# A fourth scan bank, a ring for the scan state, one block in place of two, weight turns moved, and new start and end orders

## The reference

```python
# image: patches of 16x16x3, layernorm, W, layernorm -> 196 tokens; txt gives 77 more
y = _layernorm(p, ln1_g, ln1_b)
y = jnp.einsum('bnf,fe->bne', y, W) + bias
h = jnp.concatenate([_layernorm(y, ln2_g, ln2_b), txt], axis=1)      # (32, 273, 256)
# recurrence over every second token (137 steps), state (B, 256, 64)
x_sub = x[:, ::2] * rsqrt(mean(x_sub ** 2) + 1e-6) * g_norm          # x = _layernorm(h)
x_proj, gate = jnp.split(jnp.einsum('bld,ed->ble', x_sub, w_in) + b_in, 2, axis=-1)
def step(h, xt):
    h = jnp.tanh(h * A + xt[:, :, None] * Bm)
    return (h, h @ c_sum + Dv * xt)                                    # c_sum = Cm.sum(axis=0)
out = einsum(ys * silu(gate), w_out) + b_out                           # then each row twice
h = h + out
# feed-forward on layernorm(h), int weights scaled by 1/127
return h + einsum(silu(einsum(x, wg)) * einsum(x, wu), wd)
```

## Time and profile before

| | us |
|---|---|
| median of 3 runs | 1422.66 (1420.58 to 1423.19) |
| the profiled execution | 1424.49 |
| its span, first to last instruction | 1422.6 |
| until the first `grow` | 77.2 |
| from there to the last `squash` | 1270.6 |
| from there to the end | 74.8 |

### The profile page before, as it was taken

The page is one execution under the profiler, slowest core; times in us unless marked ns, Lnnn a source line. Parts: engine busy times, 40 slices in busy tenths (PEclk is TensorE's granted clock), DMA queues, the critical chain, the costliest instruction groups (busy, mean ns, idle before and its releaser), DMA issues.

```text
span 1422.6 us, 25915 instructions
## 1 busy us (share of the span) xinstructions
PE 1248.4 (88%) x7199; PEld 642.3 (45%) x7199; DVE 1079.0 (76%) x2401; ACT 1010.4 (71%) x1955; POOL 439.5 (31%) x443
## 2 busy tenths in 40 slices
PE   3858899999999999999999999999889989988865
PEld 1623345454545454545444445454344444433333
DVE  4638788888878787878787878787888888878621
ACT  1446786868686868787878786877877778768612
POOL 5303152515161615242424343423212122121121
PEclk8769999999999999999999999999999999999987
DMA  7230414141414142332324141303232232231210
GB/s 184 65 66 19 112 29 115 32 112 33 109 33 109 45 97 62 80 78 64 88 54 104 38 111 31 98 7 108 56 89 72 55 105 56 65 81 53 53 52 7
DMA packets 154926, 100.52 MB, mean 71 GB/s; under 512 B 129088, under 2 KB 143296, under 8 KB 153536
## 3 DMA queue, kind: packets, MB, share of 16 engines
q1 hardware_dynamic: 154880, 99.95, 28.1%
HBM read 58.85 MB, written 41.06 MB: 70 GB/s over the span
## 4 chain that ended last, share of the span: by engine, by line
PE 36%; issue 22%; ACT 12%; DVE 9%; DMA 8%; POOL 6%; SPq 3%; ACTq 0%; DVEq 0%; POOLq 0%
PE U L1114 7%; PE Y L1124 7%; DVE U L693 5%; ACT h L881 4%; PE P L1259 4%; DMA y_scr<-y_fx 4%; PE P L1260 4%; PE P L1199 3%; PE P L1168 3%; PE P L1274 2%; PE P L1275 2%; DMA yT<-y_scr 2%; POOL raw_s L1006 2%; DVE act L810 2%; SPq L582 1%
## 5 line engine op out<-in xcount | busy, mean ns | idle before, releaser
L693 DVE TENSOR_TENSOR U<-h,a_col 128x512 f32<-128x512 f32 x1096 | 722.6, 690 | 182.4 <-ACT h L881 175.9
L881 ACT ACTIVATE h<-U 128x512 f32<-128x512 f32 x1096 | 626.9, 598 | 221.3 <-PE U L1114 216.8
L1114 PE MATMUL U<-x_diag,b_st 128*128 128x512 f16 x1096 | 389.8, 387 | 80.7 <-DVE U L693 68.3
L1124 PE MATMUL Y<-h,read_st 128*32 128x512 f32 x2192 | 296.5, 613 | 0.3 <-ACT h L881 0.3
L1114 PEld LDWEIGHTS U<-x_diag,b_st 128*128 128x128 f16 x1096 | 104.9, 99 | 336.3 <-DVE U L693 275.8
L1056 POOL TENSOR_TENSOR xT_act<-act,xT_act 128x448 f16<-128x448 f32 x120 | 127.7, 1071 | 196.8 <-ACT xT_act L965 196.7
L1168 PE MATMUL P<-tok_w,xT_act 128*112 128x256 f32 x672 | 171.1, 387 | 1.6 <-ACT xT_act L898 1.6
L1168 PEld LDWEIGHTS P<-tok_w,xT_act 128*112 128x112 f32 x672 | 117.8, 179 | 53.5 <-issue 21.8
L1274 PE MATMUL P<-down_w,xT_act 128*112 128x256 bf16 x480 | 114.9, 277 | 4.9 <-POOL xT_act L1056 4.9
L1275 PE MATMUL P<-down_w,xT_act 128*112 128x256 bf16 x480 | 113.7, 275 | 0.0
L810 DVE SCALAR_TENSOR_TENSOR act<-fsg,P 128x448 f32<-128x448 f32 x120 | 73.9, 615 | 41.0 <-PE P L1260 28.4
(11 more groups left out here) (136 smaller groups left out, 1485.7 us busy)
## 6 DMA issues: line engine op xcount, KB each, us to landing
raw<-in_x SPq DMA_DIRECT2D x42, 448.0 KB, 6.2
tok_scr<-tok SPq DMA_DIRECT2D x20, 448.0 KB, 3.3
gate_scr<-gate_o SPq DMA_DIRECT2D x20, 448.0 KB, 2.5
gate_fx<-gate_scr SPq DMA_DIRECT2D x20, 448.0 KB, 5.3
res<-tok_scr SPq DMA_DIRECT2D x20, 448.0 KB, 3.6
out<-res SPq DMA_DIRECT2D x76, 112.0 KB, 2.3
x_diag<-scan_scr SPq DMA_DIRECT2D x320, 16.0 KB
x_diag<-scan_scr SPq DMA_DIRECT2D x304, 12.0 KB
```

The costliest lines, as they stand in the source:

```text
L693: dve.tensor_tensor(U[bank_of(slot)][:, :].rearrange("p (l b) -> p l b", b=B), h[:, c, :].rearrange("p (l b) -> p l b", b=B), a_col[:, c * ...
L881: sc.activation(h[:, c, :], U[bank_of(slot)][:, :], ACT.Tanh, scale=1.0 / U_SCALE).then_inc(squashed, 1)
L1114: pe.matmul(U[bank_of(slot)][:, :], b_st[:, c, :], x_diag[:, c, :, t * B:t * B + B], start=False, stop=True, skip_group_check=True).then_i ...
L1124: mm = pe.matmul(Y[c4 * 32:c4 * 32 + 32, :], read_st[:, t, half, :], h[:, half * RG + c4, :], start=(j == 0), stop=(t == steps - 1), skip_ ...
```

## The change

- `NU` is 4 and there are two `P` banks. `turn` alternates between two banks. The `turn_xa` and `project` pieces share P1 with the up products, and waits are added to order them (`XA_AFTER`, `X_AFTER`, `GATE_AFTER`).
- h is a ring of 14 chunks in place of 8. PE reads a whole step (16 matmuls) at slot 3 of the next, in place of 8 matmuls every 4 slots.
- The bias of `attend` is one bf16 product of 96 rows (three bf16 parts that sum to the fp32 row) over 512 columns, in place of two fp32 products.
- One block, no barrier. ACT issues nine of the first loads. The weights are turned before the first patches are; the bias sum is done in PSUM first; the feed-forward turns move to the second iteration (`ffn_turn`, slots 37 to 55) and use P0; the maxima move to the end of the first. ACT issues half of the first `load_diag`.
- `gate_fx` is split in `gate_in` and `fx_split`, and SP loads the gate before it handles y.
- At the end: `y_next` copies the last Y inside the iteration of the last scan, the last group's residual is taken from `tok` without a trip through DRAM, the feed-forward of the last group uses the idle U banks and Y, its low parts are on DVE, and its stores are split between SP and ACT.
- Nearly every number of `PLANS` and `POOL_ORDER` is new. In the last scan's iteration the residual stands at slot 30 (before 23) and the statistics at 37 (before 23).

```diff
-READ_AT = 2
-NU = 3
+READ_AT = 3
+RING = 14
+NU = 4
...
+BIASP = 96
+XA_AFTER, X_AFTER, GATE_AFTER = 1, 2, 4
...
-        fx_low_part=(31, 37), ffn_product=(41, 51, 51, 53, 55, 55), y_copy=(2,), fx_apply=(25, 26, 27, 29),
-        fxT_copy=(38, 39), ffn_silu=(40, 43, 51, 54, 55, 55), act_high_part=(52, 52, 54, 54, 55, 55), residual=(23,)),
+        shrink=(4, 7, 8, 9, 10, 13, 15, 16), attend=(23, 25), turn_fx=(33, 37), ffn_gate=(42, 45, 49, 51, 53, 55),
...
+        residual=(30,), y_next=(50,)),
...
+        53, 54, 54, 55, 55), ffn_turn=(37, 40, 41, 43, 46, 49, 51, 54, 55, 55, 55), ffn_even=(37, 42, 46, 51, 53,
...
-        h = sb("h", [128, CHUNKS, CW])
+        bias_one = sb("bias_one", [BIASP, PT], BF16)
+        bias_row = sb("bias_row", [BIASP, D], BF16)
+        h = sb("h", [128, RING, CW])
...
-        gate_fx = sb("gate_fx", [128, 2 * DB * TOK])
-        gate_i = gate_fx[:, :].rearrange("p (a k t) -> p a k t", a=2, k=DB)
-        fx_hi, fx_lo = (gate_fx[:, n * DB * TOK:(n + 1) * DB * TOK].bitcast(FP16)
+        gate_in = sb("gate_in", [128, 2 * DB * TOK])
+        gate_i = gate_in[:, :].rearrange("p (a k t) -> p a k t", a=2, k=DB)
+        fx_split = sb("fx_split", [128, 2 * DB * TOK])
+        fx_hi, fx_lo = (fx_split[:, n * DB * TOK:(n + 1) * DB * TOK].bitcast(FP16)
                         .rearrange("p (j t) -> p j t", j=DB) for n in range(2))
...
-        P = [ctx.enter_context(nc.psum_tensor(f"P{n}", [128, 512], FP32)) for n in range(3)]
+        P = [ctx.enter_context(nc.psum_tensor(f"P{n}", [128, 512], FP32)) for n in range(2)]
...
             load_raw(sp, 0)
...
+            sp.dma_start(w_st, W.rearrange("(h k c) e -> k h c e", h=2, c=CH)).then_inc(s_w, 16)
+            for n, v in enumerate((tok_bias, ln2_g, ln2_b, b_out)):
+                sp.dma_start(rows[:, n, :], v.rearrange("(a d) -> a d", a=1).to_broadcast([PT, D])).then_inc(s_rows, 16)
             for q in range(4):
-                load(b_r[q:128:4, :, :], Bm.rearrange("(c r) s -> r c s", c=CHUNKS))
-            for n, v in enumerate((tok_bias, ln2_g, ln2_b, b_out)):
-                load(rows[:, n, :], v.rearrange("(a d) -> a d", a=1).to_broadcast([PT, D]))
-            load(cols[:, 0:4], b_in.rearrange("(k p) -> p k", p=128), allow_slow_non_contiguous=True)
-            load(cols[:, 4:6], Dv.rearrange("(k p) -> p k", p=128), allow_slow_non_contiguous=True)
-            load(cols[:, 6:8], g_norm.rearrange("(k p) -> p k", p=128), allow_slow_non_contiguous=True)
+                sp.dma_start(b_r[q:128:4, :, :], Bm.rearrange("(c r) s -> r c s", c=CHUNKS)).then_inc(s_bc, 16)
+            sp.dma_start(c_r, Cm.rearrange("(p two) s -> p (two s)", two=2)).then_inc(s_bc, 16)
...
+            sp.wait_ge(raw_in, CH * 16)
...
+        def setup_scalar_loads(sc):
+            sc.dma_start(b1, ln1_b.rearrange("(h k c) -> k h c", h=2, c=CH)).then_inc(s_w, 16)
+            sc.dma_start(cst[:, :], consts).then_inc(s_cst, 16)
+            sc.dma_start(g1, ln1_g.rearrange("(h k c) -> k h c", h=2, c=CH)).then_inc(s_w, 16)
+            sc.dma_start(w_in_r, w_in.rearrange("(k p) d -> p k d", p=128)).then_inc(s_wts, 16)
+            sc.dma_start(w_out_r, w_out.rearrange("(k p) d -> p k d", p=128)).then_inc(s_wts, 16)
+            sc.dma_start(a_r, A.rearrange("(p two) s -> p (two s)", two=2)).then_inc(s_wts, 16)
+            for c0, v in ((0, b_in), (4, Dv), (6, g_norm)):
+                sc.dma_start(cols[:, c0:c0 + v.shape[0] // 128], v.rearrange("(k p) -> p k", p=128),
+                             allow_slow_non_contiguous=True).then_inc(s_cols, 16)
...
+            pe.wait_ge(s_w, 48)
+            for f in range(KF):
+                mm = pe.matmul(Y[0:PT, 0:D], b1[:, f:f + 1].to_broadcast([128, PT]), w_st[:, f, :],
+                               start=(f == 0), stop=(f == KF - 1))
+            mm.then_inc(s_bias, 1)
...
+            tensor_body(pe, -1, general=False, **AHEAD)
...
+            pe.wait_ge(s_wts, 48)
+            for n, (blocks, _, _) in enumerate(turns):
+                if n == NU:
+                    pe.wait_ge(s_row, 1)
+                for k, src in enumerate(blocks):
+                    mm = pe.transpose(turn_of(n)[:, k * 128:k * 128 + 128], src, ident)
+                mm.then_inc(s_tr, 1)
...
-
-            if n >= 2 and n % 2 == 0:
-                pe.wait_ge(s_ffn_even, n // 2)
-            if n >= 2 and n % 2 == 1:
+                pe.wait_ge(tok_small, 26)
+            elif n % 2 == 0:
                 pe.wait_ge(s_ffn_odd, n // 2)
+            else:
+                pe.wait_ge(s_ffn_even, (n + 1) // 2)
             for k, src in enumerate(blocks):
-                mm = pe.transpose((Y, U[NU - 1])[n % 2][:, k * 128:k * 128 + 128], src, ident)
+                mm = pe.transpose(P[0][:, k * 128:k * 128 + 128], src, ident)
...
+        def gate_bank(k, scan):
+            return P[0] if scan else U[k % NU]
+
+        def up_bank(k, scan):
+            return P[1] if scan else (P[1], P[0], Y)[k % 3]
...
+                sp.wait_ge(gate_wr, (q + 1) * 16)
+                sp.sem_inc(passed, 1)
+                if due(q):
+                    sp.wait_ge(z_done, q)
+                    sp.sem_inc(passed, 1)
+                sp.dma_start(gate_in[:, :].rearrange("p (a n) -> p a n", a=2), gate_scr[q]).then_inc(gate_ld, 16)
...
-            if post:
+            if post and scan:
...
-                load_diag(sp, 0, EARLY, diag_early)
+                if not due(g):
+                    sp.wait_ge(s_clear, 3)
+                    sp.sem_inc(passed, 1)
+                    load_diag(sp, 0, EARLY, diag_early, 0, DL // 2)
+                    store_tok(sp, g, image, last_pre)
+                else:
+                    load_diag(sp, 0, EARLY, diag_early)
...
+        def store_last(sp, d, pair, hf):
+            for n in range(pair, LAST, 2):
+                sp.dma_start(out[hf * 16:hf * 16 + 16, d * ROW + n, :],
+                             tok[n // 2:n // 2 + 15 * STEPS + 1:STEPS, pair * 2 + hf, :]).then_inc(stored, 16)
...
                 dve.tensor_tensor(U[bank_of(slot)][:, :].rearrange("p (l b) -> p l b", b=B),
-                                  h[:, c, :].rearrange("p (l b) -> p l b", b=B),
+                                  h[:, (slot - CHUNKS) % RING, :].rearrange("p (l b) -> p l b", b=B),
                                   a_col[:, c * DL:c * DL + DL].unsqueeze(2).to_broadcast([128, DL, B]),
...
-            return (2, 1, 0)[n % 3]
+            return n % 2
...
-            def read_group(j, s, steps):
-
-                t, half = divmod(j, 2)
-                pe.wait_ge(squashed, s * SLOTS + (j + 1) * RG)
-                if j == 0 and due(s):
+            def read_step(t, s, steps):
+
+                pe.wait_ge(squashed, s * SLOTS + (t + 1) * CHUNKS)
+                if t == 0 and due(s):
                     pe.wait_ge(y_out, s)
-                for c4 in range(RG):
-                    mm = pe.matmul(Y[c4 * 32:c4 * 32 + 32, :], read_st[:, t, half, :], h[:, half * RG + c4, :],
-                                   start=(j == 0), stop=(t == steps - 1), skip_group_check=True)
-                if j == steps * 2 - 1:
+                for half in range(CHUNKS // RG):
+                    for c4 in range(RG):
+                        mm = pe.matmul(Y[c4 * 32:c4 * 32 + 32, :], read_st[:, t, half, :],
+                                       h[:, (t * CHUNKS + half * RG + c4) % RING, :], start=(t == 0 and half == 0),
+                                       stop=(t == steps - 1 and half == CHUNKS // RG - 1), skip_group_check=True)
+                if t == steps - 1:
                     mm.then_inc(y_ps, 1)
...
+                    pe.wait_ge(act_done, q * HB + XA_AFTER)
...
+                if image and post:
+                    pe.wait_ge(act_done, q * HB + (X_AFTER, GATE_AFTER)[part])
...
+                if k == 0:
+                    pe.matmul(P[0][0:PT, 0:2 * D], bias_one[:, :], bias_row[:, :].unsqueeze(1).to_broadcast([BIASP, 2, D]),
+                              start=True, stop=False, skip_group_check=True)
                 for j in range(DB):
                     mm = pe.matmul(P[0][0:PT, k * D:k * D + D], zT[:, j, k * PT:k * PT + PT], out_w[:, j, :],
-                                   start=(j == 0), stop=False)
-                mm = pe.matmul(P[0][0:PT, k * D:k * D + D], cst[0:PT, C_ID:C_ID + PT], rows[:, 3, :], start=False, stop=True)
...
-                if k == 0 and which == 1:
-                    if pre and image:
-                        pe.wait_ge(tok_small, g * 16 + 10)
-                    elif down:
-                        pe.wait_ge(out_done, d * 2 + 2)
-                if k > 0 and which == 0:
-                    pe.wait_ge(fsg_done, q * HB + k)
-                if k > 0 and which == 1:
-                    pe.wait_ge(act_done, q * HB + k)
+                room = 1 if scan else (NU, 3)[which]
+                if k >= room and which == 0:
+                    pe.wait_ge(fsg_done, q * HB + k - room + 1)
```

(39 more changed lines are left out.)

473 lines of the change are left out of this document (263 added, 210 removed).

## The result

The kernel after takes 1426.1 us (median of 11 runs) where the kernel before takes 1421.9: a ratio of 1.0032, 95% interval 1.0019 to 1.0044. It is 0.3% slower; the forecast was 1330 us, and the range ended at 1395. The profiled execution took 1428.1 us (span 1426.3).

The account below looks back on a forecast made before the run. The bound was taken as the scan ring's shallowness on a nearly full PE. Terms -7.7 (start), +1, -36 (image), -27 (text), -3 and -20 (end) sum to -92.7 from 1424.5, giving a median of 1330 us; range 1290 to 1395.

Parts of the forecast that it names:

- The failing step: SP's queue in every iteration: loading the 448 KB gate before y was claimed to hide, at no cost.
- The image term: Twelve image iterations: 2.4 us less each for the bank and 0.6 for the attend bias, 36 us in all.
- bias product: Attend's bias on PE: one bf16 matmul replaces four fp32 ones, saving 0.6 us per iteration.
- The fourth bank: Scan: one more slot under way cuts waits on grow, 2.4 us per image iteration and 3.9 per text iteration.
- Text iterations: Six text iterations: 3.9 us less each for the bank and 0.6 for the attend bias, 27 us in all.
- the ring: Scan's loop of grow, drive and squash, 1.7 us; a fourth slot was to remove 3.9 us per text iteration.
- The last text iteration: End of the text iterations: ln_stats four slots later avoids DVE's wait for small DMAs, -3 us beyond the general gain.
- Start: Up to the first grow: earlier patch turns -11 us, bias product +1.6, longer stretch from x_low to first drive +1.7; -7.7.
- The second iteration: Second scan iteration: it takes over eleven feed-forward turns, each waiting for the last one's copy; +1 us.
- End: Last scan iteration to the finish: earlier residual, Y and attend, cheaper bias and feed-forward, split stores, gate load; -20 us.
- The rivals: Alternatives: bank worthless 1393 us (0.17), bank fills ring 1275 (0.12), start and end fail 1355 (0.13), slower 1438 (0.05).
- the slower case: Image iterations: nine users of P1 wait for one another, costing 6 us an iteration; 1438 us, chance 0.05.

Follow-up runs that it names:

- the run with all four edits: Kernel after with y DMAs before the gate load, raw_shift at slot 38, attend at 16 and 17, maxima and bias pieces early: 1377.7 us.
- the one run meant for it: Kernel after with a_col in SBUF and the freed bank as a third P bank for the turn of xa and projections: 1552.1 us.
- the run with the maxima early: Kernel after with y DMAs before the gate load, raw_shift at slot 38, and first-part casts, maxima and bias pieces early: 1382.4 us.
- its slower ground: Kernel before with a_col in SBUF in place of PSUM: 1530.2 us; with a fourth U bank on top: 1507.4 us.

## Why the prediction was wrong

- **The failing step** is the last sentence ahead of the sum: SP's new order "waits for the gating before last and is ready long before Y, so it hides". I asked whether the gate would be ready, not what its 448 KB do to the four DMAs issued 0.6 us behind it, and who waits for those. From their issue to the loads of `yT` it took 8.7 us in place of 7.3, with the patch loads ahead of both; z came 1.6 us later in an iteration that reached `attend` 0.6 us sooner, PE, in order, stood 2.9 us and held the scan, and the products behind the pause ran at half speed. The order of the gate alone is 24 us.
- **The image term**, 12 x -3.0, came out at 43.8 us over eleven iterations and 45 to 46 over twelve. Of the eleven iterations' loss 22 us are late y and up to 14 `raw_shift` with what it freed (70.8 to 69.6). With both mended the iteration is within 1 us of the old length, not 3 us below it. By the parts (bank 1.3 and reading 0.9 by runs, bias product 0.65 by the rows) it should be nearly 3 below. No run shows what takes these 3 us, but the trace shows where PE stands. In the eleven image iterations of the run with all four edits:

```profile
PE P L1272 <- ACT xT_act L992: 8.0, 11, 1.0
PE P L1320 <- DVE act L890: 5.4, 8, 0.7
PE P L1272 <- DVE res L899: 4.5, 10, 0.5
PE P L1304 <- DVE act L890: 2.2, 8, 0.3
```

  These are waits for a P bank to be emptied, 1.8 us an iteration, and the kernel before has none of them in its eleven. The first and the third are the patch turns: with three banks a turn waited for the copy of the turn three back, with two banks for the one two back. My sum counted the users of P1 and left these out. That the 1.8 us would come back with a third bank is likely, and not shown: the one run meant for it gave no answer, since it made `grow` longer. The clock is not the cause: in the run with the maxima early these iterations have a granted clock of 0.99, as before the change, and take 69.6 us.
- **The fourth bank** was mis-sized in its reasoning. I took the 12.3 and 14.5 us for which weight loads wait for `grow` as lost time. A weight load can wait while the matmul before it still runs; PE itself waits only

```profile
PE U L1114 <- DVE U L693: 2.6, 6, 1.1
```

  in the same image iteration of the kernel before, and 3.6 in the text iteration of the earlier trace rows. My 2.4 and 3.9 asked for all of that. And the waits of the weight loads did fall by 130 us in the whole run, without a gain. In the order of the kernel before, on its slower ground, the bank brought 1.3 and 1.0. Its condition, that the order stays as good, was no part of my sum.
- **Text iterations**: 55.9 to 52.2 in the mean of four, -3.7 against -4.5 forecast (51.8 where the granted clock is 1.00). The size was nearly right and its parts were wrong, so part of that is luck: reading in one piece 1.9 and ring about 1.0 by the runs above, the bias product 0.65 by the rows (four of 0.22 against one); they add to 3.6. I had 3.9 for the ring and nothing for the reading.
- **The last text iteration**: -5.8 against -7.5, of which 4.5 were the general gain.
- **Start**: -2.2 at the first `grow` against -7.7. The turns did begin 10.6 us earlier (25.45). But seven of the patches come from POOL, which needed until 34.7 us for them, and the turns waited and ended only 2.5 us earlier; and from `x_lo` (65.07) to the first drive (84.49) it took 19.4 us, where it had been 12.5 and I had put 14 to 15: the maxima and bias pieces held the flag until 75.0, and PE came 9.5 us behind its end. The first drive is 4.2 us later than before; in return PE's stall of 7.2 us behind the third drive, which I had expected to stay, is gone. The second iteration, with the feed-forward turns, came out at +0.4 against +1.
- **End**: -15.5 against -20. The residual came 23.55 us after the last scan iteration's start (23.5 assumed), the feed-forward at 34.2 (34). The missing part is Y: its loads were issued by 1372.3 and land in 2.6 us, but POOL's order has six low parts ahead of the gating,

```profile
1379.20 4.01 POOL L1160 TENSOR_TENSOR xT_act<-act,xT_act 128x448 f16<-128x448 f32 x4 [1.13 <-ACT xT_act L1060]
1383.16 1.14 POOL L1121 TENSOR_TENSOR yT<-yT,gate_in 128x448 f32<-128x448 f32 x1
```

  so z waits for them, and I had written that "POOL's new orders only permute". The stores went on two queues at 1419.9 and took 4.8 us, as forecast.
- **The rivals**: the slower case (1438) came nearest to the measured 1426, but by luck, since its mechanism is another: its waits for P1, 6 us an image iteration, are 0.3 us in the trace:

```profile
PE P L1305 <- DVE act L891: 0.3, 1, 0.3
```

  With y and `raw_shift` mended they come to 0.7 (5.4 and 2.2 in eleven, above). I had worked out one way in which the image iteration could lose and gave it 0.05, though every slot of that iteration and an order of DMAs moved, and each loss there counts twelve times.
